# One loop body for all steps of a chunked delta-rule stage, and its inverse fetched back in pieces

## The reference, cut to what matters

```python
def step(S, xs):
    qc, kc, vc, bc = xs
    kb = kc * bc[:, None]
    A = jnp.tril(kb @ kc.T, -1)
    U = solve_triangular(eye + A, vc * bc[:, None] - kb @ S, lower=True)
    o = qc @ S + jnp.tril(qc @ kc.T) @ U
    return (S + kc.T @ U, o)
```

## Time and profile before

| what | us |
|---|---|
| median of 3 executions | 890.24 |
| lowest and highest | 885.7, 890.28 |
| the profiled execution, its own time | 894.68 |
| span of its trace | 892.8 |

### The profile page before, as it was taken

One profiled execution on the slowest core, in us unless ns is written; L12 is line 12 of the kernel. 1 busy time (PEld: TensorE's weight loads), 2 busy tenths in 40 slices (PEclk: granted clock), 3 DMA queues, 4 the chain that ended last, 5 costly groups with the idle time before them and its releaser, 6 DMA issues. The chain is left out here.

```text
span 892.8 us, 38553 instructions
## 1 busy us (share of the span) xinstructions
PE 638.5 (72%) x15734; PEld 473.7 (53%) x15734; DVE 432.8 (48%) x1547; ACT 342.3 (38%) x874; POOL 321.8 (36%) x655
## 2 busy tenths in 40 slices
PE   5777006798874757469993888888426998898984
PEld 4565005688873746259892666656312544444442
DVE  3664430123321347725553355463675656665664
ACT  4555001122220214147783344353402555554552
POOL 3577102112212730344423232542413244444433
PEclk9788555579995778579996799999855999999997
DMA  3000131111212900646552010010052323333330
GB/s 103 8 15 21 60 94 65 50 70 71 80 48 82 277 1 0 118 136 188 186 155 62 27 36 24 27 28 23 2 96 54 93 87 89 89 99 90 87 88 11
DMA packets 66572, 65.55 MB, mean 73 GB/s; under 512 B 12639, under 2 KB 56078, under 8 KB 66224
## 3 DMA queue, kind: packets, MB, share of 16 engines
q1 hardware_dynamic: 61200, 54.38, 19.9%
q0 software_dynamic: 5280, 10.00, 5.3%
HBM read 20.70 MB, written 11.93 MB: 37 GB/s over the span
## 5 line engine op out<-in xcount | busy, mean ns | idle before, releaser
L2060 PE MATMUL e_psH<-wac,e_xT 128*64 x184 | 90.5, 615 | 4.4 <-DVE e_up_w L2264 2.9
L2062 PE MATMUL e_psH<-e_up_w,e_xT 128*64 128x512 f32 x184 | 90.6, 615 | 0.0
L2007 POOL DMA_INDIRECT e_row<-xe_dram,e_read_at x46 | 44.6, 970 | 91.8 <-DVE spare L2247 65.9
L2012 POOL DMA_INDIRECT out<-spare,e_write_at x46 | 46.3, 1007 | 50.0 <-ACT spare L2137 38.5
L2081 PE MATMUL e_psY<-vb,e_hT 128*64 x368 | 51.2, 283 | 17.0 <-issue 17.0
L535 POOL TENSOR_TENSOR tb<-tinv,mb 128x128 f32<-128x128 f32 x64 | 24.3, 401 | 97.4 <-PE d_psY L545 97.4
L545 PE MATMUL d_psY<-vk_now,tb 32*32 32x48 f32 x1024 | 18.9, 226 | 54.8 <-DMA vk_now<-vk 44.4
L1193 POOL DMA_INDIRECT e_row<-xe_dram,e_read_at x39 | 37.1, 950 | 55.8 <-DVE spare L1356 37.1
L2081 PEld LDWEIGHTS e_psY<-vb,e_hT 128*64 128x64 f32 x368 | 39.9, 139 | 26.2 <-issue 26.2
L669 DVE TENSOR_TENSOR S<-d_psS,on 128x64 f32<-128x64 f32 x64 | 14.3, 223 | 80.9 <-PE d_psS L604 80.9
L2084 PE MATMUL e_psY<-e_down_w,e_hT 128*64 128x128 f32 x368 | 51.3, 284 | 0.0
(11 more groups left out here) (386 smaller groups left out, 1846.4 us busy)
## 6 DMA issues: line engine op xcount, KB each, us to landing
e_down_w<-vb SPq DMA_DIRECT2D x92, 128.0 KB
e_up_w<-wa SPq DMA_DIRECT2D x39, 256.0 KB
xe_dram<-xe SPq DMA_DIRECT2D x2, 2080.0 KB, 12.9
vk_now<-vk SPq DMA_DIRECT2D x16, 192.0 KB
kq_now<-kq SPq DMA_DIRECT2D x16, 192.0 KB
outs_dram<-spare SPq DMA_DIRECT2D x9, 256.0 KB
r<-in_L_attn_hidden_states SPq DMA_DIRECT2D x8, 256.0 KB, 4.0
gk_now<-gk SPq DMA_DIRECT2D x16, 128.0 KB
```

Source lines behind the costliest of these rows:

```text
L2007: pool.indirect_dma_start(out=row[g % ROWS][:, :], out_offset=None, in_=x_dram, in_offset=bass.IndirectOffsetOnAxis(ap=read_at[:, g:g + 1] ...
L2012: pool.indirect_dma_start(out=out, out_offset=bass.IndirectOffsetOnAxis(ap=write_at[:, g:g + 1], axis=0), in_=z[:, g], in_offset=None, bou ...
L2060: nc.tensor.matmul(psH[g % 2][0:HALF, j], xT[g % 2][:, 0:HALF], wac[:, bass.ds(who[0][j], 1)].rearrange("p a f -> p (a f)"), start=True, s ...
L2062: mm = nc.tensor.matmul(psH[g % 2][HALF:P, j], xT[g % 2][:, HALF:P], up_w[g % 2][j][:, :], start=True, stop=True)
```

## The change

SyncE reads the inverse back in 16 DMAs, one for each step (both sequences): the first two at the end of `stage_invert`, which no longer waits for them, the others from within `stage_delta`, two steps ahead, behind `kq_now`. GpSimd waits for the piece of a step before it expands it. TensorE's prologue and epilogue are gone: its loop runs over 18 passes (`STEPS = PER + 2`) of the same body, which now does `scan` of step t-2, `per_chunk` of step t-1 and `first`, `across`, `second` of step t in each pass t. In passes 0, 1, 16 and 17 part of the body works on zeros or on old data, and nobody uses what it gives. The other engines count semaphores up where they have nothing to do, S and `qe` are zeroed whole (S was zeroed in part), and SyncE's loads repeat in the last two passes.

```diff
@@ -404,6 +404,11 @@
+def inverse_in(sp, io, sb, t):
+    n = slice(t, t + PER + 1, PER)
+    sp.dma_start(sb["tinv"][:, n], io["t_dram"].rearrange("(n p) c -> p n c", p=P)[:, n]).then_inc(sb["back"][t % 4], 16)
@@ -418,7 +423,8 @@
...
-        a_in, t_set, step, turned, stored, back = (sem(n) for n in ("a_in", "t_set", "i_step", "turned", "i_stored", "i_back"))
+        a_in, t_set, step, turned, stored = (sem(n) for n in ("a_in", "t_set", "i_step", "turned", "i_stored"))
+        sb["back"] = [sem(f"i_back{i}") for i in range(4)]
@@ -430,8 +436,8 @@
...
-                sp.dma_start(sb["tinv"][:, :, :], io["t_dram"].rearrange("(n p) c -> p n c", p=P)).then_inc(back, 16)
-                sp.wait_ge(back, 16)
+                inverse_in(sp, io, sb, 0)
+                inverse_in(sp, io, sb, 1)
@@ -495,6 +501,8 @@
...
+        LEAD, STEPS = 2, PER + 2
@@ -507,26 +515,31 @@
...
-                sp.dma_start(vk_now[:, :, :].rearrange("p h c -> p (h c)"), vk[:, 0].rearrange("p b h c -> p (b h c)")).then_inc(vk_in, 16)
...
-                for t in range(PER):
-                    if t + 1 < PER:
-                        sp.wait_ge(y_ps, t + 1)
-                        sp.dma_start(vk_now[:, :, :].rearrange("p h c -> p (h c)"), vk[:, t + 1].rearrange("p b h c -> p (b h c)")).then_inc(vk_in, 16)
-                        sp.wait_ge(z_ps, t + 1)
-                        sp.dma_start(gk_now[:, :, :].rearrange("p h c -> p (h c)"), gk[:, t + 1].rearrange("p b h c -> p (b h c)")).then_inc(gk_in, 16)
+                for t in range(STEPS):
+                    n = min(t, PER - 1)
+                    if t:
+                        sp.wait_ge(y_ps, t)
+                    sp.dma_start(vk_now[:, :, :].rearrange("p h c -> p (h c)"), vk[:, n].rearrange("p b h c -> p (b h c)")).then_inc(vk_in, 16)
+                    if t:
+                        sp.wait_ge(z_ps, t)
+                    sp.dma_start(gk_now[:, :, :].rearrange("p h c -> p (h c)"), gk[:, n].rearrange("p b h c -> p (b h c)")).then_inc(gk_in, 16)
                     if t:
                         sp.wait_ge(c_ps, t)
-                        sp.dma_start(kq_now[:, :, :].rearrange("p h c -> p (h c)"), kq[:, t].rearrange("p b h c -> p (b h c)")).then_inc(kq_in, 16)
-                sp.wait_ge(kq_in, 16 * PER)
+                    sp.dma_start(kq_now[:, :, :].rearrange("p h c -> p (h c)"), kq[:, min(max(t - 1, 0), PER - 1)].rearrange("p b h c -> p (b h c)")).then_inc(kq_in, 16)
+                    if t + 2 < PER:
+                        inverse_in(sp, io, sb, t + 2)
+                sp.wait_ge(kq_in, 16 * STEPS)
+                sp.wait_ge(gk_in, 16 * STEPS)
+                sp.wait_ge(vk_in, 16 * STEPS)
...
-                pool.memset(S[:, 0], 0.0).then_inc(const, 1)
+                pool.memset(S[:, :], 0.0).then_inc(const, 1)
+                pool.memset(qe[:, :, :, :], 0.0).then_inc(const, 1)
                 pool.memset(mt[:, :, :, :], 0.0).then_inc(const, 1)
                 pool.memset(uw[:, :], 0.0).then_inc(const, 1)
                 for t in range(PER):
+                    pool.wait_ge(sb["back"][t % 4], 16 * (t // 4) + 16)
...
+                for t in range(PER, STEPS):
+                    for i, used in ((0, y_ps), (1, w_ps)):
+                        pool.wait_ge(used, t)
+                        pool.sem_inc(expanded[i], 1)
...
-                    if not start:
-                        pe.wait_ge(uw_done, t)
+                    pe.wait_ge(uw_done, t + 1)
...
-                pe.wait_ge(const, 3)
-                first(0, True)
-                across(0)
-                second(0)
-                first(1, False)
-                per_chunk(0, 0, True)
-                across(1)
-                per_chunk(0, 1, True)
-                second(1)
-                with pe.Fori(2, PER) as t:
-                    first(t, False)
-                    scan(t - 2, 0)
-                    per_chunk(t - 1, 0, False)
-                    scan(t - 2, 1)
+                pe.wait_ge(const, 4)
+                with pe.Fori(0, STEPS) as t:
+                    first(t)
+                    scan(t, 0)
+                    per_chunk(t, 0)
+                    scan(t, 1)
                     across(t)
-                    per_chunk(t - 1, 1, False)
-                    scan(t - 2, 2)
+                    per_chunk(t, 1)
+                    scan(t, 2)
                     second(t)
-                    scan(t - 2, 3)
-                scan(PER - 2, 0)
-                per_chunk(PER - 1, 0, False)
-                scan(PER - 2, 1)
-                per_chunk(PER - 1, 1, False)
-                scan(PER - 2, 2)
-                scan(PER - 2, 3)
-                for c in range(NC):
-                    scan(PER - 1, c)
+                    scan(t, 3)
...
-                for t in range(PER + 1):
+                act.sem_inc(on_done, LEAD)
+                for t in range(STEPS):
...
+                    else:
+                        act.wait_ge(y_ps, t + 1)
+                        act.sem_inc(y_sb, 1)
+                        act.wait_ge(z_ps, t + 1)
+                        act.sem_inc(z_sb, 1)
+                    if 1 <= t <= PER:
+                        act.wait_ge(c_ps, t + 1)
                         if t >= 3:
-                            act.wait_ge(s_sb, NC * (t - 2) + 1)
...
-                dve.wait_ge(const, 3)
-                dve.sem_inc(s_sb, 1)
-                dve.sem_inc(o_done, 1)
+                dve.wait_ge(const, 4)
+                dve.sem_inc(s_sb, NC * LEAD + 1)
+                dve.sem_inc(o_done, LEAD + 1)
+                dve.sem_inc(mt_done, LEAD)
+                dve.sem_inc(qe_done, LEAD)
+                dve.sem_inc(uw_done, 1)
...
+                    else:
+                        dve.wait_ge(w_ps, t + 1)
+                        dve.sem_inc(uw_done, 1)
...
-                        dve.wait_ge(on_done, t)
-                        if t >= 2:
-                            dve.wait_ge(o_ps, NC * (t - 1))
+                        dve.wait_ge(on_done, t + LEAD)
+                        dve.wait_ge(o_ps, NC * (t - 1 + LEAD))
```

More of the change, by code:

```diff
@@ L509, in _ @@
             def _(sp):
-                sp.dma_start(vk_now[:, :, :].rearrange("p h c -> p (h c)"), vk[:, 0].rearrange("p b h c -> p (b h c)")).then_inc(vk_in, 16)
-                sp.dma_start(gk_now[:, :, :].rearrange("p h c -> p (h c)"), gk[:, 0].rearrange("p b h c -> p (b h c)")).then_inc(gk_in, 16)
-                sp.dma_start(kq_now[:, :, :].rearrange("p h c -> p (h c)"), kq[:, 0].rearrange("p b h c -> p (b h c)")).then_inc(kq_in, 16)
-                for t in range(PER):
-                    if t + 1 < PER:
-                        sp.wait_ge(y_ps, t + 1)
-                        sp.dma_start(vk_now[:, :, :].rearrange("p h c -> p (h c)"), vk[:, t + 1].rearrange("p b h c -> p (b h c)")).then_inc(vk_in, 16)
-                        sp.wait_ge(z_ps, t + 1)
-                        sp.dma_start(gk_now[:, :, :].rearrange("p h c -> p (h c)"), gk[:, t + 1].rearrange("p b h c -> p (b h c)")).then_inc(gk_in, 16)
+                for t in range(STEPS):
[6 more added lines that the diff above has]
+                    sp.dma_start(gk_now[:, :, :].rearrange("p h c -> p (h c)"), gk[:, n].rearrange("p b h c -> p (b h c)")).then_inc(gk_in, 16)
@@ L547, in apply, with first @@
                     mm.then_inc(done, 1)
-                def first(t, start):
+                def first(t):
                     pe.wait_ge(vk_in, 16 * t + 16)
-                    if not start:
-                        pe.wait_ge(uw_done, t)
+                    pe.wait_ge(uw_done, t + 1)
                     pe.wait_ge(expanded[0], t + 1)
@@ L570, in second, with per_chunk @@
                     apply(1, lambda bh: zz[:, bh * RW:(bh + 1) * RW], psY, w_ps)
-                def per_chunk(t, b, start):
+                def per_chunk(t, b):
                     if b == 0:
                         pe.wait_ge(kq_in, 16 * t + 16)
[L576 to L579, removed]
+                        pe.wait_ge(on_done, t + 1)
+                        pe.wait_ge(mt_done, t + 1)
+                        pe.wait_ge(qe_done, t + 1)
                         pe.wait_ge(uw_done, t + 1)
@@ L652, in _ @@
                         act.activation(wide(zz), psZ[:, :, :], ACT.Copy, scale=mask_s[:, 1:2]).then_inc(z_sb, 1)
-                    if t:
-                        act.wait_ge(c_ps, t)
+                    else:
[5 more added lines that the diff above has]
+                        act.wait_ge(c_ps, t + 1)
                         if t >= 3:
-                            act.wait_ge(s_sb, NC * (t - 2) + 1)
-                            act.wait_ge(o_done, t - 1)
+                            act.wait_ge(s_sb, NC * t + 1)
+                            act.wait_ge(o_done, t + 1)
                         act.activation(on[(t - 1) % 2][:, :, :, :], psC[:, :, 0:B * P].rearrange("p c (b l) -> p c b l", b=B)[:, :, :, RW:RW + 2 * CH], ACT.Copy)\
@@ L663, in state @@
```

(14 more changed lines are left out.)

3 lines of the change are left out of this document (1 added, 2 removed).

## The result

The changed kernel takes 862.92 us (median of 4 runs, 861.13 to 864.28), the kernel before 889.79 in the runs beside it: ratio 0.971 (95% interval 0.968 to 0.9741). The direction was right, the size was not. The profiled executions took 864.28 and 894.68, with spans of 862.3 and 892.8.

A forecast was written before the change was run, and what follows sets the result against it. Limits differ by stretch: the inverse's DRAM round trip, TensorE in warm passes, code-page stops in the first pass and epilogue. Border 6.4 plus loop 9.5 saves 15.9 us from the 890.24 median, giving 874; range 867 to 883.

The forecast's parts named there:

- The border, 6.4 us saved: End of the inversion: SyncE issues two pieces without waiting, so TensorE may start at 129.3, 6.4 us earlier.
- Code in pages of 256 instructions, 3.95 us each when new: TensorE's code: each new page stops it 3.95 us; three stops in pass 0 put its `uw` at 13.9.
- Branches back cost no fetch: TensorE's loop: jumping back to the body fetches no code, so there are no stops from pass 1 on.
- The rival of 903: Loop: each branch back stops for a page, 17 stops of 1.7 us, 29 more; chance 0.01.
- the rule of the Trainium skill: Loop: branching breaks sequential fetch, jumps out of a two-page window stall, and kernels prefer full unrolling; it spoke against the change.
- Passes 16 and 17, and the last outputs, 13.2: Loop's end: two full passes at 6.3 us, then some 0.6 for the last sum and outputs.
- Pass 1, 9.11: Loop's second pass: code already fetched but clock still low, so 9.11 us.
- The body has the same matmuls as before, so its length stays: Loop, passes 2 to 15: 6.84 us each as before, 95.8 us in all.
- Taken as it was, 134.6: Delta stage from TensorE's start to last outputs: 132.0 us plus the earlier trace's slow clock, against 144.1 before.
- the slow phase of 2.64: Loop: the low clock seen in passes 5 and 6 of the earlier trace was assumed to recur, costing 2.64 us.
- a rival at 872: Loop: no slow clock in passes 4 to 6, 2.6 us more saved; chance 0.72 together with the main forecast.
- The rest: cost nothing: Semaphore counts, repeated loads and the stages behind: no cost, with a few us of play from clock phases.

The follow-up runs named there:

- border_only: The kernel before with the inverse fetched in 16 pieces without the wait, its prologue, loop and epilogue kept: 842.00 us, ratio 0.9925 to the kernel before.
- peel_first: The changed kernel with pass 0 written out straight ahead of a loop of 17 passes: 873.92 us, ratio 0.9821 to the kernel before.
- peel_last: The changed kernel with pass 17 written out straight behind a loop of 17 passes: 871.27 us, ratio 0.9823 to the kernel before.
- before_even: The kernel before with semaphores raised so that the waits of TensorE's loop want the same number: 840.40 us, ratio 0.9914 to the kernel before.
- after_uneven: The changed kernel with passes numbered from 2 and waits for different numbers, as before: 830.20 us, ratio 0.9818 to the kernel before.
- before_again: The kernel before, unchanged, traced afresh on a third chip: 890.58 us, ratio 0.9997.
- pad64: The changed kernel with 32 further small matmuls (64 recorded) ahead of the loop: 870.89 us, ratio 0.9767 to the kernel before.
- waits_best: The changed kernel with three implied TensorE waits per pass removed and the `uw` wait in `first` moved: 862.84 us, ratio 0.970 to the kernel before.

## Why the prediction came out as it did

- **The border, 6.4 us saved: right**, by its own steps. The start was 9.64 us after the last copy, released by `vk_now` (129.94 instead of 129.3, since that copy came 0.66 later in this execution); the pieces landed in time. border_only gives 6.4 us as a total.
- **Code in pages of 256 instructions, 3.95 us each when new: right in the main.** Three stops in pass 0, 3.88 and 3.36 apart (the idle part of each is 1.05 to 2.21 us), four q8 packets instead of twelve for the stage, `uw` at 13.79 against 13.9. The two peeled kernels put one more set of pages in at either end and pay 7.9 and 7.6 us.
- **Branches back cost no fetch: right.** No q8 packet from 146 to 256 us, over 17 branches. The rival of 903 is out, and so is, for this loop, the rule of the Trainium skill (Runtime: NRT & Kernel Launch, Instruction fetch mechanics) that speaks for it; on the contrary, the straight copies of the body in peel_first and peel_last were 7 to 10 us slower.
- **Passes 16 and 17, and the last outputs, 13.2: right**, 13.32. **Pass 1, 9.11: right**, 8.89.
- **"The body has the same matmuls as before, so its length stays": this step failed.** I took 14 x 6.84 = 95.8 us, and it is 89.67 (152.62 to 242.29, with pass 2 still partly slow at 7.20), 6.1 less. The body's matmuls are the same, but TensorE also executes its register and semaphore instructions, and they stand in the chain from `uw` to `first` and on to the next `uw`, where nothing covers them. Nothing in the earlier trace rows tells of them, since VectorE's idle time before `uw` is 0.68 before and 0.67 after; what could have told me was the built order of TensorE's instructions, in which three of them are gone and one has moved ahead of the wait, against the idle time of TensorE ahead of `first`. before_even and after_uneven give 0.38 us per pass for them, in both directions; 0.22 of it is that idle time (0.67 against 0.45). The other 0.12 of the 0.50 stays open.
- **"Taken as it was, 134.6", the slow phase of 2.64: failed.** It is in none of the traces of the new loop, and in one of four of the old. I had this as a rival at 872, and gave it no part in the number. For the stage 134.6 were forecast and 125.7 measured: 6.1 of the 8.9 are the length of the passes, 2.6 this phase.
- **"The rest: cost nothing": not right in this profile.** The stages behind took 600.6 us against 606.9, and 604.3 in before_again. Most of it goes with the granted clock of the attention stage. The seven traces with the one loop body all lie below the two of the kernel before, so something of these 3.7 to 6.3 us recurs with the change. What brings it isn't settled, the time at which the stages start, the place of their code, or the phases of the clock: pad64, which moves the code by 64 matmuls and as many loads, loses 11 in the same stretch.

The measured 26.9 us are then the 6.4 of the border (6.2 against before_again), 12.7 to 18.4 of the loop and 3.7 to 6.3 behind it, by which trace of the kernel before is taken. Its two traces put the gain in span at 23.3 and 30.5 us, one on either side of what the medians say.

## What to carry to other kernels

A loop on TensorE whose body is short matmuls paid here about 0.1 us for each register or semaphore instruction in its chain: list them engine by engine before and after an edit, not the matmuls alone, and give waits one common number by raising semaphores ahead of the loop. Straight copies of a loop's body ahead of it or behind it cost their code pages once each, and ahead of it passes at the low clock on top; a full pass on zeros inside the loop can be cheaper than either, and cheaper still when it runs under another engine's work. Before a slow phase of the clock goes into a forecast, a second trace should show it too.

## What the runs showed of the hardware

- A number worked out behind a wait, with the second semaphore instruction that this brings, cost 0.22 us on TensorE at the full clock (idle 0.67 against 0.45 before `first`). Three instructions gone and one moved give 0.38 per pass together (before_even, after_uneven), two gone 0.17 (waits_best).
- Two waits for the same number were built into one semaphore instruction, where a number to be worked out between them took a register instruction and a second semaphore instruction: a body has 275 instructions in place of 278.
- Where code lies can cost in warm passes as well, without any q8 packet: a gap of 0.10 to 0.12 us within `first`, at a fixed place of the code. What makes it is open.
- Behind the last stop for code TensorE worked on at 0.50 for 5.5 to 14.2 us in eleven traces before the clock rose, and for 18.2 in peel_first, where the stops go on for one more pass.
- With 32 small extra matmuls ahead of the loop (pad64, one trace) the stages after it took 611.8 us in place of 600.6, with the attention stage at a clock of 0.88 in place of 0.93. The cause was not tried.
